# Attention scores as three float32r products of split queries and keys, with the order of a batch written anew

## The reference

```python
h = _layernorm(x) * (1 + ca) + sa
q, k, v = split_heads(h @ Wq, h @ Wkv)                 # (32, 16, 256, 64)
s = jnp.einsum('bhid,bhjd->bhij', q * scale, k)        # the scores
gm = jnp.max(s, axis=-1, keepdims=True)                # over all keys, masked ones too
p = jnp.where(causal_mask, 0.0, jnp.exp(s - gm))
out = (p @ v) / (jnp.sum(p, axis=-1, keepdims=True) + EPS)
x = x + ga * (out @ Wo + bo)
h = _layernorm(x) * (1 + cb) + sb
gate, up = fp4(h) @ fp4(w_gate).T, fp4(h) @ fp4(w_up).T
x = x + gb * (fp4(silu(gate) * up) @ fp4(w_down).T)
```

## Time and profile before

| what | value |
|---|---|
| median of 3 runs | 1296.12 us (1295.63 to 1296.16) |
| the profiled execution's own time | 1295.38 us |
| its span, first to last instruction | 1293.6 us |
| granted TensorE clock, mean | 0.989 of 2.4 GHz |
| busy share of the span | PE 96%, DVE 76%, ACT 69%, POOL 66% |

### The profile page before, as it was taken

The page is one execution under the profiler, slowest core; times in us unless marked ns, Lnnn a source line. Parts: engine busy times, 40 slices in busy tenths (PEclk is TensorE's granted clock), DMA queues, the critical chain, the costliest instruction groups (busy, mean ns, idle before and its releaser), DMA issues.

```text
span 1293.6 us, 34330 instructions
## 1 busy us (share of the span) xinstructions
PE 1247.5 (96%) x10194; PEld 1023.9 (79%) x10194; DVE 985.3 (76%) x2461; ACT 898.1 (69%) x2988; POOL 853.9 (66%) x1595
## 2 busy tenths in 40 slices
PE   6999999999999999999999999999999999999973
PEld 4778888888888878888878888888888888888853
DVE  5577877777878777878777877777787777787863
ACT  6776776777776777766777777777677777677640
POOL 4757676667676666766666766667766666767653
PEclk9999999999999999999999999999999999999995
DMA  3000000000000000000000000000000000000000
GB/s 104 20 20 24 18 6 23 22 22 22 16 10 18 22 22 22 20 6 18 22 22 22 22 11 11 22 22 22 22 16 6 22 22 22 22 16 6 19 20 10
DMA packets 38920, 26.53 MB, mean 21 GB/s; under 512 B 2896, under 2 KB 34128, under 8 KB 38896
## 3 DMA queue, kind: packets, MB, share of 16 engines
q1 hardware_dynamic: 38480, 25.96, 7.1%
q10 hardware_dynamic: 416, 0.26, 0.1%
HBM read 21.94 MB, written 4.28 MB: 20 GB/s over the span
## 4 chain that ended last, share of the span: by engine, by line
PE 94%; DVE 2%; ACT 2%; POOL 1%; issue 1%; DMA 0%; POOLq 0%; DVEq 0%; ACTq 0%
PE ps_m L1037 25%; PE ps_s L1136 19%; PE ps_m L1011 18%; PE ps_o L1166 14%; PE ps_m L1089 9%; PE ps_s L1146 5%; PE ps_m L1113 3%; ACT probs L659 1%; ACT qk L617 0%; DVE neg_max L861 0%; POOL qy L75 0%; POOL qy L73 0%; POOL probs L451 0%; DMA x_in<-L_attn_x 0%; POOL hq L77 0%
## 5 line engine op out<-in xcount | busy, mean ns | idle before, releaser
L659 ACT ACTIVATE probs<-ps_s,neg_max 128x128 f32<-128x128 f32 (+1 forms) x1024 | 424.1, 433 | 182.1 <-PE ps_s L1146 180.5
L451 POOL TENSOR_SCALAR probs<-probs,r_den 128x256 f32<-128x256 f32 (+1 forms) x768 | 354.9, 479 | 0.0
L861 DVE TENSOR_REDUCE neg_max<-ps_s 128x4 f32<-128x1024 f32 x256 | 305.6, 1215 | 61.1 <-PE ps_s L1136 61.1
L449 POOL TENSOR_TENSOR probs<-probs,r_den 128x128 f32<-128x128 f32 x256 | 107.3, 419 | 308.0 <-DVE r_den L872 293.8
L1136 PE MATMUL ps_s<-qk 64*128 64x256 f32 x2048 | 265.0, 394 | 1.8 <-ACT probs L659 1.8
L613 ACT COPY probs_t<-ps_m 128x512 f32<-128x512 f32 x288 | 168.5, 606 | 120.8 <-PE ps_m L1011 120.6
L1011 PE MATMUL ps_m<-ident,probs 128*128 128x128 f32 x1536 | 235.8, 277 | 7.1 <-ACT qk L617 3.6
L1136 PEld LDWEIGHTS ps_s<-qk 64*128 64x128 f32 x2048 | 183.0, 187 | 61.7 <-issue 32.5
L659 ACT ACTIVATION_READ_ACCUMULATOR probs<-ps_s,neg_max 128x1 f32 x1024 | 221.0, 216 | 0.0
L1011 PEld LDWEIGHTS ps_m<-ident,probs 128*128 128x128 f32 x1536 | 172.2, 140 | 40.4 <-ACT qk L617 13.4
L1166 PE MATMUL ps_o<-probs_t,v 128*64 128x256 f32 (+1 forms) x2048 | 194.7, 332 | 3.6 <-ACT probs_t L613 1.9
(11 more groups left out here) (111 smaller groups left out, 1787.6 us busy)
## 6 DMA issues: line engine op xcount, KB each, us to landing
mod_a<-mod_rows SPq DMA_DIRECT2D x32, 256.0 KB, 3.4
x_res<-L_attn_x SPq DMA_DIRECT2D x32, 128.0 KB, 2.1
out<-y_out SPq DMA_DIRECT2D x32, 128.0 KB, 1.8
x_in<-L_attn_x SPq DMA_DIRECT2D x31, 128.0 KB, 2.1
mod_b<-mod_rows SPq DMA_DIRECT2D x32, 64.0 KB, 2.9
wkv<-L_attn_Wkv SPq DMA_DIRECT2D x3, 256.0 KB, 6.0
wo<-L_attn_Wo SPq DMA_DIRECT2D x1, 512.0 KB, 5.6
wkv<-L_attn_Wkv SPq DMA_DIRECT2D x2, 128.0 KB, 3.7
```

The lines of the kernel that those rows point to most:

```text
L449: nc.gpsimd.tensor_tensor(cols, cols, r_den[:, u % 4, 0:1].to_broadcast([P, P]), ALU.mult)
L451: ins = nc.gpsimd.tensor_scalar(cols, cols, r_den[:, u % 4, s:s + 1], 1.0, ALU.mult, ALU.mult)
L659: ins = nc.scalar.activation(probs[:, u % 4, h, t * P:(1 + 2 * t) * P], ps_s[:, 2 * (u % 2) + h, t * N:t * N + (1 + t) * P], ACT.Exp, bias ...
L861: nc.vector.tensor_reduce(neg_max[:, u % 4, :], ps_s[:, 2 * (u % 2):2 * (u % 2) + 2, :].rearrange("p b (t j) -> p (b t) j", t=2), AX.X, AL ...
```

## The change

The projected queries and keys are now kept as two float32r tiles, `qk_r[0]` (high, written by ScalarE from PSUM) and `qk_r[1]` (low, written by VectorE as PSUM less the high part). A unit's scores become twelve float32r matmuls in place of four float32 ones. A `qk` step's bank is free, and a unit's scores may begin, when VectorE has written the low part. All five engines but SyncE get a new order within the batch; which steps ScalarE and which VectorE reads changes, their numbers don't (VectorE reads three `t` steps and copies `ps_o` twice per batch, as before). The core of the diff:

```diff
-        qk = sb("qk", [P, 4, 2, N])
+        qk_r = [sb(f"qk_r{n}", [P, 4, 2, N], F32R) for n in range(2)]
...
         SHARED = (
-            (("xqt", 2, 0), "t0", "qk0", "t1", "qk1", ("gate", 2, 0), ("v", 0, 0), ("v", 0, 1), "t2", ("up", 2, 0), ("gate", 2, 1)),
-            ("t0", "qk0", "qk1", ("up", 2, 1), ("wo", 1, 0), "t1", ("wo", 1, 1), ("hqt", 2, 0), "t2", ("v", 0, 2)),
-            (("hqt", 2, 1), ("down", 2, 0), "qk0", "t0", "qk1", "t1", ("v", 0, 3), ("xt", -1, 0), "t2"),
-            ("t0", "qk0", "qk1", ("down", 2, 1), "t1", "t2"))
+            (("xqt", 2, 0), "t0", "qk0", "qk1", ("gate", 2, 0), ("v", 0, 0), ("up", 2, 0), "t1", "t2", ("gate", 2, 1)),
+            ("qk0", ("up", 2, 1), ("wo", 1, 0), "qk1", ("wo", 1, 1), ("v", 0, 1), "t0", "t1", "t2", ("hqt", 2, 0)),
+            (("down", 2, 0), ("v", 0, 2), "qk0", "t0", "qk1", ("hqt", 2, 1), ("v", 0, 3), "t1", "t2", ("xt", -1, 0)),
+            ("t0", "t1", "qk0", "qk1", ("down", 2, 1), "t2"))
...
 # ScalarE, shared_reads
                 elif kind == "qk":
                     act.wait_ge(qk_full, UNITS * b + k + 1)
-                    nc.scalar.copy(qk[:, k % 4, :, :], ps_m[bank][:, :].rearrange("p (n j) -> p n j", n=2)
-                                   ).then_inc(qk_ready, 1)
+                    nc.scalar.copy(qk_r[0][:, k % 4, :, :], ps_m[bank][:, :].rearrange("p (n j) -> p n j", n=2)
+                                   ).then_inc(qk_high, 1)
...
 # VectorE, shared_reads
+                    elif kind == "qk":
+                        dve.wait_ge(qk_high, UNITS * b + k + 1)
+                        nc.vector.tensor_tensor(qk_r[1][:, k % 4, :, :], ps_m[bank][:, :].rearrange("p (n j) -> p n j", n=2),
+                                                qk_r[0][:, k % 4, :, :], ALU.subtract).then_inc(qk_ready, 1)
...
 # TensorE, scores(u)
                     for t in range(2):
-                        for h in range(2):
-                            rows = slice(h * DH, (h + 1) * DH)
-                            mm = nc.tensor.matmul(ps_s[:, 2 * (u % 2) + h, t * N:(t + 1) * N],
-                                                  qk[rows, u % 4, 0, t * P:(t + 1) * P], qk[rows, u % 4, 1, :],
-                                                  start=(t == 0), stop=True, skip_group_check=True)
+                        for n, (l, r) in enumerate(((0, 1), (1, 0), (0, 0))):
+                            for h in range(2):
+                                rows = slice(h * DH, (h + 1) * DH)
+                                mm = nc.tensor.matmul(ps_s[:, 2 * (u % 2) + h, t * N:(t + 1) * N],
+                                                      qk_r[l][rows, u % 4, 0, t * P:(t + 1) * P], qk_r[r][rows, u % 4, 1, :],
+                                                      start=(t == 0 and n == 0), stop=(n == 2), skip_group_check=True)
```

More of the change, by code:

```diff
@@ L556, in body @@
                             round_weights(1)
+                        keep()
                         normalize(i, 0)
+                        round_hidden(i - 2, 0)
+                        residual()
                     elif j == 1:
-                        keep()
                         normalize(i, 1)
@@ new lines, in body @@
+                        shared_reads(0, 2)
+                        shared_reads(0, 3)
+                        shared_reads(0, 4)
+                        shared_reads(0, 6)
+                        hidden_scales(i - 2, 0)
+                        shared_reads(0, 7)
+                        shared_reads(0, 9)
+                        denominators(0)
+                    elif j == 1:
+                        maxima(2)
+                        hidden_magic(i - 2, 0)
+                        shared_reads(1, 1)
+                        shared_reads(1, 0)
+                        maxima(3)
@@ L935, in body @@
                         denominators(1)
-                        maxima(2)
-                        maxima(3)
-                        hidden_magic(i - 2, 0)
+                        hidden_scales(i - 2, 1)
+                        shared_reads(1, 2)
                         shared_reads(1, 3)
-                        hidden_scales(i - 2, 1)
+                        denominators(2)
                         shared_reads(1, 4)
-                        denominators(2)
-                        shared_reads(1, 6)
@@ L944, in body @@
-                        hidden_magic(i - 2, 1)
+                        attended_stats()
                         if i_is(i, 1):
-                            shared_reads(1, 7)
+                            shared_reads(1, 9)
                     elif j == 2:
                         input_stats()
-                        attended_stats()
+                        denominators(3)
+                        attended_normalized()
                         maxima(4)
+                        hidden_magic(i - 2, 1)
@@ L959, in body @@
+                        denominators(4)
+                        out_copy()
+                        ffn_in_scales()
+                        if i_is(i, 1):
+                            shared_reads(2, 5)
                     elif j == 3:
-                        attended_normalized()
+                        denominators(5)
                         maxima(6)
                         h_low_part()
-                        denominators(5)
+                        maxima(7)
+                        ffn_in_magic()
@@ L964, in body @@
+                        shared_reads(3, 1)
+                        denominators(6)
+                        shared_reads(3, 2)
                         out_copy()
-                        maxima(7)
-                        ffn_in_scales()
-                        denominators(6)
                         shared_reads(3, 3)
-                        ffn_in_magic()
+                        shared_reads(3, 4)
                     if i_is(i, 0) and j == 0:
@@ L1005, in _ @@
             value_low_part(0)
+            for n, place in enumerate(((3, 2), (3, 3))):
+                dve.wait_ge(qk_high, n + 1)
+                nc.vector.tensor_tensor(qk_r[1][:, n, :, :], ps_m[shared_steps(-1)[place][3]][:, :].rearrange("p (n j) -> p n j", n=2),
+                                        qk_r[0][:, n, :, :], ALU.subtract).then_inc(qk_ready, 1)
             iterations(dve, body)
@@ L1186, in body @@
                         at_place(0, 4)
+                        mask(0, 1)
+                        mask(1, 0)
+                        mask(1, 1)
                         at_place(0, 5)
@@ L1211, in body @@
                         mask(4, 0)
+                        mask(4, 1)
                         at_place(2, 0)
-                        mask(4, 1)
                         at_place(2, 1)
@@ L1236, in _ @@
             shared = shared_steps(-1)
-            for place in ((2, 7), (3, 1), (3, 2)):
+            for place in ((2, 9), (3, 2), (3, 3)):
                 shared_step(*shared[place][0:4])
```

106 lines of the change are left out of this document (47 added, 59 removed).

## The result

The changed kernel takes 1322.59 us (median of 4 runs, 1321.06 to 1323.16), the kernel before, run beside it, 1296.14 (1295.63 to 1297.1). The ratio is 1.020, 95% interval 1.0188 to 1.0213: 26.5 us slower, where 13.6 less were forecast. The profiled execution took 1323.16 us for a span of 1321.4.

What follows compares the result with a forecast made beforehand. TensorE was taken to bound the kernel at 38.54 us per batch. VectorE would then set the pace: undisturbed 34.9 plus waits 2.8 plus 0.4 stretched gives 38.1, 0.44 less x 31 = 13.6 us: 1282.5 us, range 1256 to 1312.

Steps and rivals of the forecast that it cites:

- TensorE's scores: Score products on TensorE: 1.62 us per j instead of 1.93, 1.24 us less per batch.
- Rival D: Score halves not side by side in float32r, or weight loads exposed: 1432 or 1513 us; chance 0.04.
- The subtraction: Eight per batch on VectorE: 692 ns each, 0.61 us of its queue, 4.9 us per batch.
- The new waits: VectorE waits in j = 2, before attended_normalized, and at up of j = 0 and j = 1: together 2.8 us per batch.
- the third of the stretches: Of 1.3 us VectorE time in stretched instructions, a third (0.4) adds to the batch; waits swallow the rest.
- 31.3 + 4.9 = 36.2: VectorE's time per batch: 38.54 less 7.2 of waits gives 31.3, plus 4.9 for the subtractions.
- P = 38.1: Forecast batch period in us, 0.44 below the 38.54 before.
- Its other work moves but doesn't grow: VectorE's work besides the subtractions stays at 31.3 us per batch in the new order.
- Rival C: Slower kernel: VectorE's waits for ScalarE's high parts add to its own time, up to 2.8 us, 1310 us; chance 0.31.
- the gain of TensorE: Shorter scores bring TensorE alone to 37.3 us per batch; 38 us in all if nothing else held it up.
- Start and end: Work before and after the steady batches: 0 change counted, 2 us either way; two extra subtractions ahead, 1.4 us at most.
- TensorE's 0.8 us idle: Sign that the forecast was right: TensorE idle about 0.8 us per batch, released by VectorE.

Runs made afterwards that it cites:

- e17: Old engine order, scores as three float32r products of high parts alone, no subtraction (low parts left out); 1284.23 us, ratio 0.9911 to the kernel before.
- e14: Changed kernel's order, three products of high parts alone, no subtraction, ScalarE's copy frees the bank; 1291.83 us, ratio 0.9969 to the kernel before.
- e9: Changed kernel with three of eight subtractions halved (qk1 of j = 2, qk0 and qk1 of j = 3), keys' low part alone in the products; 1320.86 us.
- e10: Changed kernel with the read of t1 in j = 0 moved from VectorE to ScalarE; 1318.0 us, ratio 1.0166 to the kernel before.
- e7: Changed kernel with input_normalized ahead of the qk1 subtraction in j = 2 and VectorE's two ps_o copies given to ScalarE; 1326.64 us, ratio 1.0243.
- e19: Changed kernel's order and handover, subtracting 192 of 256 columns, products of high parts alone; 1315.14 us, ratio 1.0148 to the kernel before.
- e3: Changed kernel's new order with the old float32 scores and no subtraction; 1306.74 us, ratio 1.0092 to the kernel before.
- e16: Changed kernel's order, waits and releases, subtracting only 8 of 256 columns, products of high parts alone; 1291.17 us, ratio 0.9962 to the kernel before.
- e1: Changed kernel subtracting for the keys alone; the product with the queries' low part replaced by a second with the keys' low part; 1295.81 us.
- e5: Changed kernel with input_normalized called before the qk1 subtraction in j = 2, full computation; 1316.66 us, ratio 1.0161 to the kernel before.
- e15: New order, high-part products, no handover; each subtraction replaced by a 432-column SBUF-to-SBUF one nobody waits for; 1345.84 us, ratio 1.0389 to the kernel before.
- e18: New order, high-part products, no handover; each subtraction replaced by a 512-column maximum with one SBUF input; 1310.47 us, ratio 1.0108 to the kernel before.

## Why the prediction was wrong

**TensorE's scores: right.** 1.62 us a `j`, with the two halves side by side and the loads hidden. Rival D, and with it the load rule of the Trainium skill, "TensorE: Matmul & The Clock Gate", Part 3 (The mechanism), is not what these rows show: 24 loads of 0.19 us, 4.5 in sum, take 1.62 us together with their products, and the three products of a half use the same rows. The same section also has loads into a background weight buffer pulled ahead of running matmuls; the trace agrees with that part.

**The subtraction: right.** 684 ns, 692 forecast. I counted 0.61 of the queue for each, by the overlap of back-to-back instructions, and that is what it takes:

```profile
678.86 0.69 DVE L812 TENSOR_TENSOR qk_r<-ps_m,qk_r 128x512 fp32r<-128x512 f32 x1
679.46 0.68 DVE L883 COPY o_t<-ps_o 128x512 f32<-128x512 f32 x1
680.06 0.68 DVE L812 TENSOR_TENSOR qk_r<-ps_m,qk_r 128x512 fp32r<-128x512 f32 x1
680.66 0.28 DVE L840 TENSOR_TENSOR ffn<-ps_m,mod_b 128x128 f32<-128x128 f32 x1
```

From the start of each subtraction to the start of the next instruction, waits left out, the eight of a batch sum to 4.90 us (mean of batches 10 to 25), 4.9 forecast.

**The new waits: right in place, smaller in sum.** The subtraction of `qk1` in `j = 2` begins 2.35 us after the end of `maxima(5)` (667.97), 2.45 forecast; it waits 0.8, not 1.2, since `y_out` ahead of it takes 0.61. `attended_normalized` waits 0.4 (0.4 forecast), `up` of `j = 0` 0.5 (0.4), `up` of `j = 1` 0.2 (0.6). In all 2.1 of the 2.8. After the third of the stretches I had charged 1.9.

**The step that failed is VectorE's own time, "31.3 + 4.9 = 36.2".** Counted in the same way, as the period less the waits that the profile lists (idle over 0.15 us), it is 39.33 - 2.1 = 37.2 after, 1.0 more. The waits are 2.1, where 1.9 were charged. That is the 1.2 by which P = 38.1 fell short. Of the 1.0, 0.6 is a wait that I counted twice. The window behind the earlier trace rows holds the first maxima of its own batch and, by 0.01 us, those of the next, each with its wait of 0.54:

```profile
626.63 1.22 DVE L861 TENSOR_REDUCE neg_max<-ps_s 128x4 f32<-128x1024 f32 x1 [0.54 <-PE ps_s L1136]
...
665.16 1.23 DVE L861 TENSOR_REDUCE neg_max<-ps_s 128x4 f32<-128x1024 f32 x1 [0.54 <-PE ps_s L1136]
```

A batch waited 6.6 us, not 7.2, and VectorE's own time was 31.9, not 31.3. The other 0.4 is "Its other work moves but doesn't grow": it grew from 31.9 to 32.3. The order alone can make it grow: with no subtraction and the same instructions own time is 31.8 in e17 and 32.9 in e14, and VectorE is busy for 30.3 and 31.1.

The prediction has the same sum in a second form: undisturbed durations 34.9, waits 2.8 and "a third" of the 1.3 of stretched time, 0.4. Measured against the same 34.9, the waits are 2.1 and the stretched time is 2.3, of which 0.7 are made good by the smaller waits and 1.6 add. The third was the part called most likely to be wrong. With 31.9 in the place of 31.3 the same working gives 38.3 (34.9 + 2.8 + a third of 1.9), still faster than before; the double count alone did not turn the forecast. With 37.5, which stood beside 36.2 as the upper end, and the 1.9 of waits the sum would have been 39.4. Rival C named the direction and the price ("up to the whole 2.8: P = 39.0"); the measured 39.3 is beyond it.

**The stretched instructions moved; they didn't vanish.** `scale` fell from 500 ns to 300, `y_out` rose from 345 to 579, two a batch: +0.47 against -0.40. What stretches them is GpSimd, as in e9: the `scale` of the earlier trace rows ends 0.04 us after the GpSimd instruction that it lies beside. Such time is a wait for GpSimd that no view of waits lists, and I took it for VectorE's own.

**But that sum is bookkeeping.** It closes for each kernel by construction, and it doesn't say what a change will do. The experiments say that where VectorE loses work, its waits or the times that GpSimd holds it grow: e10 exchanges 1.1 us busy (0.66 of it the copy) for 1.0 waiting, e9 gets back nothing, e7 gets longer, e19 has 0.4 less busy time and 0.2 less period. And one thing I had not put up as a rival was true: **the gain of TensorE was never there to be had in full.** With the shorter scores, and nothing added on VectorE, the old order comes to 38.21 (e17) and the new to 38.55 (e14), where I had TensorE alone at 37.3. Of the 1.24 us, 0.33 was real. From there VectorE's load takes 0.76 in the new order (39.31 against e14's 38.55), and the order itself 0.34 (e14 against e17; 0.46 with float32 scores, e3). -0.33 + 0.34 + 0.76 = +0.77 a batch. The prediction put the order at nothing, without a reason. The split rests on differences between whole runs, so the 0.76 includes whatever the subtractions move elsewhere.

**Start and end: wrong.** 0 with 2 us either way was forecast; the start cost 4.0 beyond its periods, 3.3 of them by a wait of TensorE in the batches ahead of the loop and the slower clock behind it. e16 has both with almost nothing subtracted, so it isn't the "two more subtractions ahead, 1.4 us at most".

**The chain of work gives no price.** Its shares in the kernel after, and in e1:

```profile
POOL 47%; issue 30%; DVE 12%; PE 7%; ACT 2%; POOLq 2%; DMA 0%; DVEq 0%
```

```profile
POOL 47%; issue 30%; DVE 12%; PE 8%; ACT 2%; POOLq 2%; DMA 0%; DVEq 0%
```

Read alone, it says GpSimd. The two kernels are 0.81 us a batch apart with the same shares, so it doesn't tell what the subtractions cost, and in its longest "issue" pieces (2.5 to 3.2 us) GpSimd was waiting for the denominators, as the view of the waits in the one batch says:

```profile
POOL probs L450 <- DVE r_den L877: 11.0, 6, 3.2
```

The two engines hold each other up: VectorE by the reciprocals that GpSimd waits for, GpSimd by holding VectorE's instructions. No run took work off GpSimd, so how much of the period its holds set was not tested.

**A sign that told nothing:** TensorE's 0.8 us idle came true, and the period missed by 1.2. Busy time of pipelined matmuls stretches with the batch, 38.56 us here for steps that add up to 37.3. By my own list an idle time over 1.3 was to mark the slower case; it was slower at 0.8.

**What stays open.** Which loops through the engines hold 38.2 to 38.5 with TensorE's steps at 37.3, and why the step from half to three quarters of the load costs 0.60 and the next 0.21. Links tight to 0.1 or 0.2 us in the batch after are GpSimd's second rounding (ends 669.63) with `hqt` of `j = 2` (669.77) and `up` with VectorE; three attempts to loosen such places gave -0.14, -0.19 and +0.33 a batch. No kernel that keeps the whole computation beat the kernel before: e3, with the scores left in float32, is 0.9% behind, and of those with split scores e5 comes nearest, 1.6% behind. Whether an order exists that carries eight full subtractions at 38.5 was not settled.

## What to carry to other kernels

When a change moves work from the bounding engine to another, the room on the other is not its waits: small gaps stay, a wait taken by new work comes back elsewhere, and part of its busy time may be time in which a third engine holds it. Here 8.2 us not busy out of 38.54 took about 3.4 us of new work (e1) at a time level with before, and that with TensorE's scores shorter by 1.2 us a batch. When waits are summed over a window of one period, see that the wait at its edge is counted once. Before counting on the bounding engine's gain, run it with the new work left out (e17, 12 us of 38) in the old order; that says what there is to pay with. Cost the written-out iterations ahead of a loop on their own: the handover, which cost nothing within the loop, made a 2.2 us wait there (e16), and a slower clock came on top.

## What the runs showed of the hardware

**Two SBUF inputs on VectorE slow GpSimd.** Beside e15's load GpSimd's 128x352 product takes 1051 ns and its `probs` 561; beside e18's, 932 and 514; without any (e14) 933 and 509. The subtraction from PSUM, with one input in SBUF, leaves them alone (933 and 512 in the kernel after). The batch is 1.16 us longer with it (40.31 against 39.15), of which the load's own greater length, 8 x 0.06, can make 0.5. The Trainium skill, "SBUF — State Buffer" (Who interferes with whom), says the same: a VectorE instruction with two SBUF inputs contends with a GpSimd instruction that reads SBUF, one with at most one such input, outside the two-port modes, does not. The trace agrees on both.

**It goes the other way too, by where instructions fall.** `xn` of the input, the same instruction, takes 415 ns before, 436 after, 621 in e14, 733 in e18. Where it meets a GpSimd instruction it ends 0.15 us after that one's end (after, e9, e14 and e18 alike), whether it began 0.32 us into it or 0.06; alone it takes 0.34. `scale` and `den_eps`, which have one input, can be held as well and then end 0.02 to 0.04 us after; whether they run in a two-port mode no run shows. e18's 39.15 contains the longer `xn`, 0.6 us a batch against the kernel after, so that it isn't a pure price of the load either.

**float32r products on two halves of the rows** run side by side as float32 ones do: 24 of them with 24 weight loads, 256 columns each, in 1.62 us. One after another, at the 0.118 us of a `qk` product, they would take 2.8.
